# Two products in one pass for the router's and layer 3's factor columns, small matrices used in place, and the first phase begun in setup

## The reference

```python
# per layer: four modulated convolutions over positions, 32 -> 32 channels, 3 taps:
#   'same', 'upsample' (+ blur), 'same', (blur +) 'downsample'
s = style @ mw.T + mb
weight = SCALE * w * s[:, None, :, None]
demod = lax.rsqrt(jnp.sum(weight * weight, axis=(2, 3)) + EPS)
out = conv(x, weight * demod) + b

# linear layer 0: W + mixed low-rank weights        (folded into one 512x512 matrix in setup)
# linear layer 1: W_base, router over E=8 experts, top 2 by softmax, rank-16 adapter each
# linear layer 2: kernel + per-sample and shared low-rank weights
# linear layer 3: W_up, gate over 4 experts, top 1, rank-8 adapter each
# out = x + linear(conv(x))
```

## Time and profile before

| What | us |
|---|---|
| median of 3 runs (1299.99 to 1307.54) | 1300.73 |
| the profiled execution's own time | 1306.01 |
| its span, first to last instruction | 1304.2 |
| TensorE busy in the span | 1233.0 |
| TensorE idle in the span | 71.2 |
| mean granted clock of TensorE | 0.987 of full |

### The profile page before, as it was taken

One profiled execution on the slowest core, in us unless ns is written; L12 is line 12 of the kernel. 1 busy time (PEld: TensorE's weight loads), 2 busy tenths in 40 slices (PEclk: granted clock), 3 DMA queues, 4 the chain that ended last, 5 costly groups with the idle time before them and its releaser, 6 DMA issues.

```text
span 1304.2 us, 45847 instructions
## 1 busy us (share of the span) xinstructions
PE 1233.0 (95%) x21400; PEld 704.6 (54%) x21400; DVE 496.3 (38%) x975; ACT 356.1 (27%) x757; POOL 546.2 (42%) x417
## 2 busy tenths in 40 slices
PE   5847999999999999999999999999999999999997
PEld 5323556555555555565565555565565554665555
DVE  5612324344333333434333333434333434433343
ACT  2213313223322222313223222312323222312321
POOL 3156641444443442644323543644413544634400
PEclk9968999999999999999999999999999999999999
DMA  8232300002221200000301300000211200000101
GB/s 285 114 105 101 115 17 2 2 3 59 98 105 62 99 3 2 3 2 25 134 27 42 131 3 2 2 2 13 103 53 58 99 3 2 2 2 3 67 2 65
DMA packets 20828, 65.66 MB, mean 50 GB/s; under 512 B 4032, under 2 KB 4416, under 8 KB 16160
## 3 DMA queue, kind: packets, MB, share of 16 engines
q1 hardware_dynamic: 18960, 60.85, 12.8%
q10 hardware_dynamic: 1680, 1.89, 0.5%
HBM read 43.85 MB, written 18.87 MB: 48 GB/s over the span
## 4 chain that ended last, share of the span: by engine, by line
PE 87%; DVE 4%; POOL 1%; issue 1%; ACT 0%; DMA 0%; DVEq 0%; POOLq 0%
PE bank_b L1137 26%; PE bank_a L1068 13%; PE bank_a L1052 11%; PE bank_b L1052 11%; PE bank_b L1003 8%; PE bank_b L1095 5%; PE bank_a L1078 5%; PE bank_a L1027 3%; PE bank_b L1149 2%; PE bank_b L1118 1%; DVE w_sum L957 1%; PE bank_b L1130 1%; POOL xs L716 1%; POOL sum_v L698 1%; DVE z L939 1%
## 5 line engine op out<-in xcount | busy, mean ns | idle before, releaser
L698 POOL TENSOR_TENSOR sum_v<-raw_v 128x768 f32<-128x768 f32 x32 | 58.9, 1842 | 626.5 <-ACT raw_v L760 626.5
L1137 PE MATMUL bank_b<-w_hi,y3t_hi 128*128 128x512 f32 x512 | 210.0, 410 | 12.4 <-DVE w_sum L957 12.1
L1137 PE MATMUL bank_b<-w_hi,y3t_lo 128*128 128x512 f32 x512 | 203.0, 396 | 2.2 <-issue 2.2
L1137 PE MATMUL bank_b<-w_lo,y3t_hi 128*128 128x512 f32 x512 | 202.4, 395 | 0.1
L1068 PE MATMUL bank_a<-y,w_down 64*32 64x512 f32 x3072 | 173.6, 594 | 1.5 <-ACT wv L762 1.5
L1052 PE MATMUL bank_a<-y,wv 32*64 32x512 f32 (+2 forms) x3584 | 145.8, 480 | 2.3 <-issue 2.3
L1052 PE MATMUL bank_b<-y,wv 32*64 32x512 f32 (+2 forms) x3584 | 142.3, 480 | 1.8 <-ACT y L741 1.8
L895 DVE TENSOR_TENSOR x<-bank_b,x 128x512 f32<-128x512 f32 x96 | 66.4, 692 | 202.2 <-PE bank_b L1137 166.0
L753 ACT ACTIVATE y<-bank_a,cb,tab 128x512 f32<-128x512 f32 x64 | 49.7, 776 | 319.4 <-PE bank_a L1068 319.4
L1003 PE MATMUL bank_b<-xs,cw 32*32 32x512 f32 x3072 | 112.0, 615 | 15.3 <-POOL xs L716 15.3
L1137 PEld LDWEIGHTS bank_b<-w_hi,y3t_hi 128*128 128x128 f32 x512 | 96.8, 189 | 50.9 <-DVE w_sum L957 15.6
(11 more groups left out here) (172 smaller groups left out, 1553.0 us busy)
## 6 DMA issues: line engine op xcount, KB each, us to landing
w_hi<-w_scratch SPq DMA_DIRECT2D x9, 1024.0 KB, 5.8
w_lo<-w_scratch SPq DMA_DIRECT2D x9, 1024.0 KB, 8.0
x_in<-in_x SPq DMA_DIRECT2D x32, 256.0 KB, 4.1
out_x<-out_tile SPq DMA_DIRECT2D x32, 256.0 KB, 2.4
w_raw<-w_scratch SPq DMA_DIRECT2D x3, 1024.0 KB, 9.8
w_scratch<-w_hi SPq DMA_DIRECT2D x3, 1024.0 KB, 3.9
w_scratch<-w_lo SPq DMA_DIRECT2D x3, 1024.0 KB, 6.9
w<-in_w SPq DMA_DIRECT2D x2, 1024.0 KB, 13.5
```

The source lines that it names most:

```text
L698: ins = g_.tensor_tensor(dst[:, :, at:at + count].rearrange("p r k o -> p r (k o)"), src[:, :, 0:count].rearrange("p r k o -> p r (k o)"), ...
L1137: ins = pe.matmul(lin_ps[b][:], y3t[yi][:, k, P * b:P * (b + 1)], w[use(m) % 2][wi][:, k], start=(k == 0 and i == 0), stop=(k == KB - 1 an ...
```

## The change

- **Two products in one pass.** The router's columns stand twice in the weights, hi and lo (`r1`, 16 columns), and so do layer 3's (`a3`, 128 columns). Each is multiplied with `y3t` hi and `y3t` lo: 8 matmuls in place of 12. The two halves come out in different rows, and VectorE adds them after the turn: one more instruction in layer 1, two more in layer 3 (`z_sum`, 4 x 64 columns).
- **Turned parts of 128 rows.** `logits` has 128 rows (16 used, the rest zeroed once), and each of its four turns is 128 x 128.
- **Block-diagonal matrices gone.** `wq` and `bias_q` are dropped; the matmuls take 32 x 32 pieces of `sq` and `bias_w` in place, four for one before.
- **First phase begun in setup.** `w2s`, products, their copies, `xs`, blur, `conv0` and the first evacuation `y0` of phase 0 run in setup, between the work on layer 0's weights and layer 2's factors; main starts with `conv2(0, 0)`. GpSimd's adds on `w0` stand behind the blur. SP loads `x_in` before `w0`, `b2`, `a2`, `w2`. Setup's table, `up` and bias instructions are reordered on VectorE, and the copies of `down` go to ScalarE.
- **Summing phases.** `effective(m, 0)` stands right behind `base(m, 0)` on TensorE, ahead of `products(n + 1)` and `base(m, 1)`, and on VectorE right behind `residual(m, 0)`.

```diff
-Z1 = E1 * R1 + E1
+Z1 = E1 * R1 + 2 * E1
...
+            act.wait_ge(keep["pr_done"], 1)
+            for r in range(ROWS):
+                a.activation(raw_v[:, r, 1:RAW + 1].rearrange("p k o -> p (k o)"), w2_ps[r][:, 0:RAW * CH],
+                             ACT.Copy).then_inc(keep["raw_ready"], 1)
...
+            pool.wait_ge(scale_ready, 1)
+            g.tensor_tensor(w2s[:], cw[:, 2, 0].rearrange("p t o -> p (t o)").unsqueeze(1)
...
+            for b in range(ROWS):
+                pool.wait_ge(keep["x_loaded"][b], 16)
+                g.tensor_tensor(xs[:, b, 1:LEN + 1], keep["x_in"][:, b], column(T_S, b).broadcast_to((P, LEN)),
+                                ALU.mult).then_inc(keep["xs_ready"], 1)
...
-            pe.wait_ge(wq_ready, ROWS)
+            pe.wait_ge(sum_ready, 1)
             pe.wait_ge(square_ready, 1)
             for l in range(LAYERS):
                 for i, k in enumerate(SIDES):
                     out = var_last_ps[:, l] if i == 4 else var_ps[:, l, i]
-                    last = pe.matmul(out, wq[:, CONVS * l + k], mod_sq[:, l, i], start=True, stop=True)
+                    for r in range(ROWS):
+                        rows = slice(CH * r, CH * (r + 1))
+                        last = pe.matmul(out[rows], sq[rows, l, k, 0], mod_sq[rows, l, i], start=True, stop=True)
...
+            pe.wait_ge(up_ready, 1)
+            pe.wait_ge(keep["w2s_ready"], 1)
+            pe.wait_ge(mod_ready, 3)
+            product_tiles(pe, w2_ps, keep, 0).then_inc(keep["pr_done"], 1)
...
+            pe.wait_ge(keep["xs_ready"], ROWS)
...
+            conv0_tiles(pe, w2_ps, keep, 0).then_inc(keep["c0_done"], 1)
...
+                ps, columns, weights_ = (logit_ps, 2 * E1, keep["r1"]) if l == 1 else (z_ps, 2 * Z23, keep["a3"])
+                for k in range(KB):
+                    for yi in range(2):
+                        ins = pe.matmul(ps[0:columns], weights_[:, k], y3t[yi][:, k],
+                                        start=(k == 0 and yi == 0), stop=(k == KB - 1 and yi == 1))
...
-                        ins = pe.transpose(logit_ps[:, E1 * t:E1 * (t + 1)], logits[:, tokens], ident[0:E1, 0:E1])
+                        ins = pe.transpose(logit_ps[:, tokens], logits[:, tokens], ident[:])
...
+                    parts = logit_ps[:].rearrange("p (t c) -> p t c", c=P)
+                    then(v.tensor_copy(lg[:], parts[:, :, 0:e]))
+                    then(v.tensor_tensor(lg[:], lg[:], parts[:, :, e:2 * e], ALU.add))
...
+                    then(v.tensor_copy(z_sum[:], parts[:, :, 0:Z23]))
+                    then(v.tensor_tensor(z_sum[:], z_sum[:], parts[:, :, Z23:2 * Z23], ALU.add))
...
                     residual(m, 0)
+                    effective(m, 0)
                     residual(m, 1)
-                    effective(m, 0)
...
                     base(m, 0)
+                    effective(m, 0)
                     if adapts:
                         to_tokens(m)
                         base(m, 1)
-                        effective(m, 0)
```

More of the change, by code:

```diff
@@ L53 @@
 PAD = 2
+ON_ACT, ON_DVE = (0, 2), (1, 3)
 DOWN = (
@@ L61, with product_tiles, conv0_tiles @@
 DOWN_FACTORS = (0.125, 0.375)
+def product_tiles(pe, banks, keep, l):
+    for s, at, first, count in (*((t, CH * t, 0, TAPS) for t in range(TAPS)),
+                                (TAPS, RAW * CH, TAPS - 1, 1), (TAPS + 1, (RAW + 1) * CH, 0, 1)):
+        for d in range(ROWS):
+            for r in range(ROWS):
+                rows, c = slice(CH * r, CH * (r + 1)), (r + d) % ROWS
+                last = pe.matmul(banks[r][CH * c:CH * (c + 1), at:at + count * CH], keep["up"][rows, l, s],
+                                 keep["w2s"][rows, (r + c) % ROWS, first * CH:(first + count) * CH],
+                                 start=(s == 0), stop=True, skip_group_check=True)
+    return last
+def conv0_tiles(pe, banks, keep, l):
+    for t in range(TAPS):
+        for d in range(ROWS):
+            for r in range(ROWS):
+                rows, c = slice(CH * r, CH * (r + 1)), (r + d) % ROWS
+                last = pe.matmul(banks[r][CH * c:CH * (c + 1)], keep["cw"][rows, 0, l, t],
+                                 keep["xs"][rows, (r + c) % ROWS, t:t + LEN],
+                                 start=(t == 0), stop=(t == TAPS - 1), skip_group_check=True)
+    return last
 def setup_program(nc, ctx, io, keep, scratch):
@@ L342, in _ @@
-            dve.wait_ge(blocks, 2 * TAPS)
-            for g in range(ROWS):
-                rows = slice(CH * g, CH * (g + 1))
-                v.tensor_copy(keep["down"][rows], w_dn[rows, :, TAPS * (g % 2):TAPS * (g % 2 + 1)])
+            v.tensor_copy(keep["up"][:, :, 0:TAPS], cw[:, 1])
+            for i, (large, small_) in enumerate(((0, 1), (2, 1))):
+                ins = v.scalar_tensor_tensor(out=keep["up"][:, :, TAPS + i], in0=cw[:, 1, :, large], scalar=-3.0,
+                                             in1=cw[:, 1, :, small_], op0=ALU.mult, op1=ALU.subtract)
@@ L474, in _ @@
             pe.wait_ge(loaded["b2"], 16)
-            pe.wait_ge(w0_copied, KB)
+            pe.wait_ge(bias_copied, 2)
             g2 = gmat[:].rearrange("p k b r -> p k (b r)")
             for banks, raw, done in ((b2_ps, b2, b2_done), (a2_ps, a2, a2_done)):
+                if done is a2_done:
+                    pe.wait_ge(loaded["as2"], 16)
+                    pe.wait_ge(loaded["bs2"], 16)
+                    pe.wait_ge(keep["y0_act"], 2)
+                    pe.wait_ge(keep["y0_dve"], 2)
+                    for p in range(KB):
+                        pe.matmul(w2_ps[p], as2[:, p * P:(p + 1) * P], bs2[:], start=True, stop=True).then_inc(w2_done, 1)
                 for h in range(2):
@@ L708, in _ @@
                 src = x[g] if l else x_in
-                for b in range(ROWS):
+                for b in range(ROWS if n else 0):
                     if l:
@@ L995, in _ @@
         def _(pe):
-            def unit(banks, l, taps, done):
-                for i, (weights, block_, src, shift) in enumerate(taps):
-                    for d in range(ROWS):
-                        for r in range(ROWS):
-                            rows, c = slice(CH * r, CH * (r + 1)), (r + d) % ROWS
-                            ins = pe.matmul(banks[r][CH * c:CH * (c + 1)],
-                                            weights[rows, l, block_],
-                                            src[rows, (r + c) % ROWS, 1 + shift:1 + shift + LEN],
-                                            start=(i == 0), stop=(i == len(taps) - 1), skip_group_check=True)
-                ins.then_inc(done, 1)
             def conv0(n):
```

322 lines of the change are left out of this document (161 added, 161 removed).

## The result

The changed kernel takes 1270.17 us (median of 4 runs, 1269.14 to 1273.94) against 1301.1 for the kernel before on the same chip: a ratio of 0.9758, 95% interval 0.972 to 0.9795. It is 31 us faster where 51.5 were forecast, and 1270 lies outside 1240 to 1262. Its profiled execution took 1269.14 us with a span of 1267.3.

What follows compares the result with a forecast made beforehand. TensorE, busy for 1233.0 of 1304.2 us, was taken as the bound. The terms 14.8 + 3.2 - 0.3 + 12.1 + 21.7 = 51.5 us, off the 1300.7 median, gave 1249 us, range 1240 to 1262.

Steps and rivals of the forecast that it cites:

- Change 1: Router and layer 3 products: twelve passes to eight, 64 matmuls fewer at 0.232 us each, 14.8 us gained.
- change 2: Layer 1's turns of 128 rows: chain starts 0.6 earlier, extra instruction costs 0.2; 0.4 per phase, 3.2 us gained.
- Change 3: Summing phases: `effective(m, 0)` moved ahead removes all eight TensorE waits for `w_sum`, 12.1 us gained.
- Change 4: Phase 0 begun in setup: main starts at 67.2 with `conv2`, 21.7 us gained, bounds 14 and 26.
- The sums `sq` are ready at 17.18: Setup, VectorE: start of the rebuilt chain, the sums' time taken from the profile of before.
- I allow ... and take 21.0: Setup, TensorE: 160 small variance matmuls end at 21.0, 7.7 earlier; 19.7 if as fast as the products' matmuls.
- I put `conv0` at 39: Setup, TensorE: phase 0's `conv0` starts at 39 (38 to 41), after bias products waiting for VectorE's partly slowed instructions.
- The drop of the clock in main's first `conv2`: Start of main: the fall to 1.2 GHz after the idle between programs is paid by `conv2`, costing 1.9 us.
- Setup grows: Rival in setup: small pieces don't run side by side, TensorE stays at its lower level; gain 37.5, 1263 us; chance 0.09.
- Gains turn into waits: Rival in the loop: layer 1's chain late or longer, or `xs` swallows part of the `w_sum` gain; 1262 us; chance 0.07.
- Not faster: Rival at the turn back in 16 adapter phases: new wait drops TensorE's clock each time; 1279 us at 1.9 each; chance 0.03.
- three signs of being wrong: Main starting after 72, the clock's mean under 0.97, or new waits for `xs` beyond phase 1.

Runs made afterwards that it cites:

- x8: x6 with the router's four turns 16 x 16 again instead of 128 x 128, same matmul count; 1260.76 us, ratio 0.9674.
- x1: The kernel before with the two-in-one passes, 128-row turns and new summing order, but setup, block-diagonal matrices and phase 0 as before; 1279.31 us, ratio 0.9825.
- x2: The changed kernel plus 32 tiny matmuls (128 instructions, half a block) in setup ahead of TensorE's wait for the sums; 1263.60 us, ratio 0.9707.
- x3: The changed kernel plus 64 tiny matmuls (256 instructions, a full block) at the same place in setup as x2; 1274.26 us, ratio 0.9781.
- x6: x2 plus 18 more tiny matmuls (72 instructions) ahead of phase 15's first convolution; 1256.04 us, ratio 0.9639.
- x5: The kernel before, unchanged, run again for a second profile; 1298.80 us (one run).
- x7: x6 with the setup order of x4; 1252.50 us, ratio 0.9609.
- x4: The changed kernel with VectorE's bias weights moved ahead of its variance wait and GpSimd's gate matrix behind phase 0's `xs`; 1270.66 us, ratio 0.976.
- x11: x7 with GpSimd's two multiplications on layer 0's `b` held back until VectorE's squares and sums are done; 1251.68 us, ratio 0.9597.
- x12: x7 with SP's 2 MB load of layer 0's next weights moved behind the output stores of the same loop step; 1253.05 us, ratio 0.9615.

## Why the prediction was wrong

- **Change 1 and change 2: right.** The router's products and layer 3's are 128 matmuls at 0.23 us, as reckoned. A layer 1 phase lost 1.34 (reckoned 0.93 + 0.40), a layer 3 phase 0.88 (0.93). x8 gives 0.65 for the wide turns, against the 0.6 that I had for the earlier start of VectorE's chain; the 0.2 of its extra link belongs to change 1. The wait for `z` came with 0.5 each where 0.4 was named.
- **Change 3: right, a little small.** 14.2 for 12.1. I priced the waits by their own length, 1.51 each, and a phase pays 1.77 for one. What the other 0.26 is, no run takes apart.
- **Change 4: the term that was mis-sized**, 21.7 where x1 and x2 show 15.7, and the profiles of before and after 11.9 at the first turn. Its steps: "The sums `sq` are ready at 17.18" failed by 2.2, since GpSimd's work on `b` came to stand beside VectorE's squares. "I allow ... and take 21.0" gave the matmuls 3.8 us; by themselves they took 2.6 (19.46 to 21.80, and 0.26 at the end), the products' pace. What had no term was the 3.56 us of waiting for a block of instructions among them: forty matmuls of the trace had become 160, 240 instructions more in 2 us, and a boundary fell among the last. Another 2.2 us of the same kind fell into the products at 39.4. "I put `conv0` at 39" failed by 6.3 for these reasons together and for the bias weights, whose slowing I had named but not priced. The drop of the clock in main's first `conv2` was put at 1.9 and came to 7.12 - 4.44 = 2.7.
- **The step that was missing.** No term of the sum, and no rival, asked what adding and removing instructions does to TensorE's instruction blocks. "Four fewer in each of 8 layer 1 phases and 8 layer 3 phases" took away time and also moved every boundary behind it. The loop's excess went from about 10 us at the median of before (an estimate) to 20.1, so this alone took some 10 us from the gain. x2, x3 and x6 show that these move with the count alone. The trace of before held the signs, with idle times ended by "issue" at L1027, L1052 and L1137 (7.4 us together), which I had passed over.
- **The account.** Between the two profiled executions: 51.5 forecast, -9.8 for the start (21.7 reckoned, 11.9 seen at the first turn; 6 of it at equal places, by x1 and x2, the rest again stalls at boundaries, such as 2.15 us in the first products of main), +1.4 for the undisturbed loop and the last phase (31.2 for 29.8), -6.2 for the loop's excess. That is 36.9, which is what they differ by (1306.01 and 1269.14). The medians differ by 31 since the profile of before lay 5 us above its median and that of the changed kernel 1 below. I had set the forecast against the median without asking what the 5 us were; x5 shows that they were excess.
- **The rivals.** "Setup grows" gave 1263 and has the right part of the kernel, but its mechanism is not what happened: L522's 16 matmuls took 9.98 us, as L463's 9.82, so nothing was added there. "Gains turn into waits" has the right form and the wrong waits. "Not faster" needed the clock to fall at each turn back; the wait of 0.5 left the matmuls behind it at 0.23, and even of the changed kernel's six idle times of 1.5 us and more in the loop only one, 1.85 us, was followed by a fall. Of the three signs of being wrong that the prediction named, one came: main started at 73.9, after 72. The mean clock, 0.989, and the waits for `xs` showed nothing.
- With the places moved twice and the setup order mended, the same change gives 1252.50 (x7), 0.9609 of before, 50.8 us less by its own comparison.

## What to carry to other kernels

- Idle time of TensorE ended by "issue" isn't noise: count instructions, see if it stands at multiples of 256, and look at what used up the block before it. Hundreds of tiny matmuls in a row are where it hurts; long matmuls between them hide it, if what depends on them has slack. A block can also come late because data are on the DMA engines.
- An edit that adds or removes matmuls moves all boundaries behind it. Compare variants by the lengths of undisturbed phases, and try the finished kernel with a few tiny matmuls as a shift. Here it was worth 14 us, about as much as the change that took out 64 matmuls (14.8 by the forecast, which the phases bear out).
- On a chain with several late parts, mending one may show nothing (x4, x11) or be lost until the other is mended too (x7).

## What the runs showed of the hardware

- TensorE's instructions come in blocks of 256, each packet mostly taking 0.9 to 1.4 us here. Two to two and a half microseconds of products used one up, which cost a stall of 0.4 to 2.3 us in the changed kernel's loop. In setup, with the DMA engines busy (share 1.03 from 14 to 26 us), it was 3.56 us, and 4.26 in x3. TensorE went on 1.2 to 1.6 us after the packet had landed, in 120 stalls of fourteen traces.
- Data hold a packet back: behind the same boundary it started after 3.14 us at a DMA share of 0.97 (x7) and after 1.23 us at 0.02 (x12), and so, to one side or the other, at all seven boundaries where the two kernels differ in it. In setup it started 3.9 to 4.1 us behind the boundary at 15 us in x2, x7 and x11 (share 1.07 to 1.08), whether TensorE's variance products had begun at 19.10, 18.62 or 17.24.
- A stall of 1.85 us was followed by 3 us at a granted clock of 0.51, so it cost about 1.5 us more than its own length (nine matmuls 0.43 apart in place of 0.23, less the start). Stalls of 2.31, 2.23 and 2.16 us in the same loop were not followed by a fall. What decides it stays open.
- Stalls at the same boundary differ between executions by up to 1.3 us (1.26 us at 437 in the profile of before, none at that place in x5). Between these two executions 6.0 of 7.2 us were excess.
- **Still open:** what else sets the moment at which a block's packet starts. Behind 80 us in the changed kernel the median is 0.8 us after the boundary where the data take less than half of the DMA engines in the microsecond behind it (144 boundaries), and 2.9 us where they take more (19). But 22 of the 144 packets started over 3 us late as well.
